# First latent scores ahead of the scan's last sums: query pairs issued inside the scan, the second half's output, norm and latents between the scores, the window masks on GpSimd

## The reference, cut to what matters

```python
# 4th part, cut: a linear recurrence over time
x_proj = x @ proj_in_w.T + proj_in_b
delta = softplus(x_proj @ B_w.T)                      # 16 states
h = h * sigmoid(A) + x_t[:, :, None] * d_t[:, None, :]  # scan over t
y_t = h.sum(axis=1) @ C_w.T + D_param * x_t
x = layernorm(x + (y @ proj_out_w.T + proj_out_b + x))
# 5th part, cut: cross-attention with latents, 16 heads
kv_c = kv @ W_kvc;  q_c = q @ W_dq
q = q_c @ W_uq, rope(q_c @ W_qr);  k, v from kv_c
good = (k_ids <= seg_id) & (k_ids >= seg_id - 8)
attn = softmax(where(good, q.k * scale, -1e30))
out = (attn @ v) @ W_o
```

## Time and profile before

| | us |
|---|---|
| median of 3 runs | 761.76 (760.17 to 761.87) |
| the profiled execution | 763.71 |
| its span, first to last instruction | 761.9 |
| TensorE busy in the span | 698.1 (92%) |
| VectorE busy | 485.4 (64%) |
| GpSimd busy | 318.7 (42%) |
| ScalarE busy | 305.6 (40%) |

### The profile page before, as it was taken

The page is one execution under the profiler, slowest core; times in us unless marked ns, Lnnn a source line. Parts: engine busy times, 40 slices in busy tenths (PEclk is TensorE's granted clock), DMA queues, the critical chain, the costliest instruction groups (busy, mean ns, idle before and its releaser), DMA issues.

```text
span 761.9 us, 12253 instructions
## 1 busy us (share of the span) xinstructions
PE 698.1 (92%) x4554; PEld 534.4 (70%) x4554; DVE 485.4 (64%) x928; ACT 305.6 (40%) x716; POOL 318.7 (42%) x453
## 2 busy tenths in 40 slices
PE   5989899999999898777999999999979999999993
PEld 4856564685666565435877787877858888888883
DVE  4478764331135789975998988882455656565656
ACT  3655523102211845122767776771142222222220
POOL 4323316400101769402766666662243445544521
PEclk9999999999799999887999999999979999999998
DMA  7000006001002000000000000003010111121001
GB/s 261 1 2 3 2 2 274 1 0 42 1 1 78 1 18 1 1 1 0 2 1 1 2 1 2 2 0 105 1 41 22 52 54 42 43 63 42 1 0 56
DMA packets 10460, 23.28 MB, mean 31 GB/s; under 512 B 2081, under 2 KB 5218, under 8 KB 10018
## 3 DMA queue, kind: packets, MB, share of 16 engines
q1 hardware_dynamic: 10402, 22.50, 8.9%
HBM read 21.45 MB, written 1.05 MB: 30 GB/s over the span
## 4 chain that ended last, share of the span: by engine, by line
PE 74%; DVE 18%; ACT 4%; issue 3%; DMA 1%; POOL 0%; POOLq 0%; DVEq 0%; SPq 0%; ACTq 0%
PE psum L394 30%; PE psum L427 8%; DVE A L1259 7%; PE psum L914 6%; PE psum L945 4%; PE psum L646 4%; PE psum L923 3%; PE psum L450 3%; PE psum L729 2%; PE psum L501 2%; PE psum L543 1%; DVE probs L1103 1%; DVE A L1170 1%; PE psum L507 1%; PE psum L407 1%
## 5 line engine op out<-in xcount | busy, mean ns | idle before, releaser
L394 PE MATMUL psum<-parts 128*128 128x256 f32 (+2 forms) x1440 | 255.8, 337 | 13.5 <-DVE parts L1124 8.7
L394 PEld LDWEIGHTS psum<-parts 128*128 128x128 f32 (+1 forms) x1440 | 221.4, 194 | 45.6 <-DVE parts L1124 8.7
L1710 POOL TENSOR_SCALAR probs<-probs,row_rec 128x256 f32<-128x256 f32 x128 | 60.8, 489 | 55.0 <-DVE row_rec L1114 53.9
L1433 ACT ACTIVATE probs<-probs,neg_max 128x256 f32<-128x256 f32 x128 | 64.0, 503 | 40.4 <-DVE neg_max L1107 40.4
L1259 DVE TENSOR_TENSOR_SCAN A<-decay,psum 128x256 f32<-128x256 f32 x128 | 75.0, 660 | 5.4 <-PE psum L774 5.4
L1660 ACT ACTIVATE A<-psum 128x512 f32<-128x512 f32 x44 | 26.3, 598 | 129.6 <-PE psum L394 129.6
L1380 DVE TENSOR_TENSOR A<-A,psum 128x512 f32<-128x512 f32 x44 | 30.2, 687 | 70.2 <-PE psum L394 70.2
L1826 POOL CAST parts<-C 128x512 fp32r<-128x512 f32 (+1 forms) x44 | 31.1, 707 | 100.5 <-PE psum L394 90.1
L914 PE MATMUL psum<-C,A 128*128 128x256 f32 x256 | 69.6, 396 | 0.0
L1827 POOL TENSOR_TENSOR parts<-C,parts 128x512 fp32r<-128x512 f32 (+1 forms) x44 | 54.9, 1247 | 3.5
L914 PEld LDWEIGHTS psum<-C,A 128*128 128x128 f32 x256 | 44.8, 194 | 15.6 <-issue 10.7
(11 more groups left out here) (206 smaller groups left out, 1191.1 us busy)
## 6 DMA issues: line engine op xcount, KB each, us to landing
C<-in_experts SPq DMA_DIRECT2D x22, 384.0 KB, 3.1
A<-in_w_o SPq DMA_DIRECT2D x1, 2048.0 KB, 12.0
x_tok<-in_x_tok SPq DMA_DIRECT2D x1, 1024.0 KB, 6.9
ctxT<-in_ctxT SPq DMA_DIRECT2D x1, 1024.0 KB, 10.4
out<-x_tok SPq DMA_DIRECT2D x8, 128.0 KB, 1.8
A<-in_w_uqT SPq DMA_DIRECT2D x1, 768.0 KB, 6.0
xT<-in_xT SPq DMA_DIRECT2D x2, 256.0 KB, 4.4
C<-in_wqk SPq DMA_DIRECT2D x1, 512.0 KB, 5.8
```

The costliest lines, as they stand in the source:

```text
L394: ins = mm(o, left[l], right[r], start=first and n == 0, stop=last and n == 2, skip_group_check=True)
L1433: last = af(slot, scores, ACT.Exp, bias=neg_max[:, u % RING[n], j:j + 1], accum_out=row_sum[:, u % RING[n], j:j + 1])
L1710: last = pool.tensor_scalar(pr, pr, row_rec[:, u % RING[n], j:j + 1], 1.0, ALU.mult, ALU.mult)
```

## The change

Pairs 0 to 2 are issued by TensorE in units 29 to 31 of the scan and pair 3 right behind; the scores begin when scan 62 of 64 is through. The last state sums and the second half's `outputs` come after `scores4(1)`, its output products after scores 2 and 3, its turn after scores 9, its query latents after scores 13. VectorE rotates pairs 0 and 1 inside the scan and does merge, residuals, norm and `query_low(1)` inside the attention. The eight masks are written by GpSimd in the odd units 7 to 21 of the scan, behind a wait for `k_tok`. `latents_by_token` turns the keys' latents instead of multiplying again. The first half's output products, norm, turn and latents come one unit earlier. ScalarE loads its exponential table in unit 20. The second half's sums go to a place of their own, and some PSUM banks change.

```diff
-        FIRST = 3
-        QUERIES_AT = {2 * (n - FIRST) + 1: n for n in range(FIRST, B * NPAIR)}
+        FIRST = 4
+        QUERIES_AT = {2 * (n - FIRST) + 4: n for n in range(FIRST, B * NPAIR)}
+        TURNS_AT, LATENTS_AT = 9, 13
 # TensorE
             def latents_by_token():
-                pe.wait_ge(sem("k_latT"), 2)
+                pe.wait_ge(sem("k_latT"), 4)
                 for i in range(NT):
-                    for c in range(DC):
-                        last = mm(bank[4][:, KVC * i:KVC * i + KVC],
-                                  ctxT[:, i // 2, c, (i % 2) * P:(i % 2 + 1) * P], w_kvc[:, c, 0:KVC],
-                                  start=(c == 0), stop=(c == DC - 1))
+                    last = pe.transpose(bank[4][:, KVC * i:KVC * i + KVC], keys_b[0:KVC, i * P:(i + 1) * P],
+                                        ident[0:KVC, 0:KVC])
...
-                if n == 22:
+                if n == 21:
                     final(3, (2, 3), out3)
-                if n == 26:
+                if n == 25:
                     ln_transposes(3, 0)
-                if n == 28:
+                if n == 27:
                     query_latents(0)
-            state_sums(7)
-            pe.wait_ge(sem("q_split"), 3)
-            pe.wait_ge(sem("operand_lo"), QC_AT + 1)
+                if n == 29:
+                    pe.wait_ge(sem("q_split"), 3)
+                    pe.wait_ge(sem("operand_lo"), QC_AT + 1)
+                if n >= 29:
+                    query_pair(n - 29)
+            query_pair(3)
+            def next_queries(u):
+                n = QUERIES_AT.get(u)
+                if u == 1:
+                    state_sums(7)
+                    outputs(1)
+                if u in (2, 3):
+                    if u == 2:
+                        pe.wait_ge(sem("q_mul"), 3)
+                    final(3, (2 * u, 2 * u + 1), out3)
+                if u == min(QUERIES_AT):
+                    pe.wait_ge(sem("ln_r"), 8 * 3 + NT)
+                if u == TURNS_AT:
+                    pe.wait_ge(sem("q_mul"), QUERIES_AT[u - 1] + 1)
+                    pe.wait_ge(sem("q_lat"), QUERIES_AT[u - 1] + 1)
+                    ln_transposes(3, 1)
+                if u == TURNS_AT + 1:
+                    pe.wait_ge(sem("ln_xT"), 4 * 3 + 4)
+                if u == LATENTS_AT:
+                    pe.wait_ge(sem("q_mul"), QUERIES_AT[u - 1] + 1)
+                    query_latents(1)
+                if u == LATENTS_AT + 1:
+                    pe.wait_ge(sem("operand_lo"), QC_AT + 2)
+                if n is not None:
+                    query_pair(n)
...
-            query_pair(0)
-            outputs(1)
-            query_pair(1)
-            pe.wait_ge(sem("q_mul"), 1)
-            final(3, range(4, NT), out3)
-            query_pair(2)
-            pe.wait_ge(sem("q_lat"), 3)
-            ln_transposes(3, 1)
-            query_latents(1)
-            pe.wait_ge(sem("q_mul"), 3)
+            pe.wait_ge(sem("s_scan"), 2 * SCAN_UNITS - 2)
             pe.wait_ge(sem("k_add"), 4)
 # VectorE, in the scan (residual3(2), (3) at m == 43, normalise at 47, query_low(0) at 57)
+                if m in (60, 62):
+                    rotate_pair((m - 60) // 2)
-            window_mask(0)
-            rotate_pair(0)
-            merge(1)
-            rotate_pair(1)
-            for i in range(4, NT):
-                residual3(i)
             rotate_pair(2)
-            for i in range(4, NT):
-                normalise(3, i)
-            window_mask(1)
-            query_low(1)
+            rotate_pair(3)
+            dve.wait_ge(sem("mask"), NT)
 # VectorE, rotate_next(u) of the attention
-                if u % 16 in (10, 12) and u < 16 * (B - 1):
-                    window_mask(2 * (u // 16) + 2 + u % 16 // 12)
+                if u == 1:
+                    merge(1)
+                if u in (2, 3):
+                    for i in (2 * u, 2 * u + 1):
+                        residual3(i)
+                if u == 5:
+                    for i in range(4, NT):
+                        normalise(3, i)
+                if u == LATENTS_AT:
+                    query_low(1)
 # ScalarE
+                if n == 20:
+                    af(small[:, 0, 0:1], small[:, 1, 0:1], ACT.Exp)
+                if n >= 30:
+                    latent_pair(n - 30)
+            latent_pair(2)
+            latent_pair(3)
             sums_out(1)
...
+                if u == TURNS_AT:
+                    ln_out(3, 1)
+                if u == LATENTS_AT:
+                    query_high(1)
 # GpSimd
+            def window_mask(i):
+                link(pool.tensor_scalar(distance, iota4, seg_f[:, i:i + 1], 1.0, ALU.subtract, ALU.mult))
+                link(pool.tensor_tensor(distance, distance, distance, ALU.mult))
+                pool.tensor_scalar(mask_m[:, i, :], distance, 16.0, NEG, ALU.is_gt, ALU.mult).then_inc(sem("mask"), 1)
+                pool.wait_ge(sem("mask"), i + 1)
-                if n == 25:
+                if n == 24:
                     rstd_of(3, (0,))
+                if n == 7:
+                    loaded(pool, "iota4", "seg")
+                    link(pool.tensor_copy(seg_f[:, :], seg_i[:, :]))
+                    pool.wait_ge(sem("k_tok"), 1)
+                if n % 2 and 7 <= n < 7 + 2 * NT:
+                    window_mask((n - 7) // 2)
+                if n == 31:
+                    add_pair(0)
...
+                if u == 4:
+                    rstd_of(3, (1,))
-            add_pair(0)
-            add_pair(1)
-            rstd_of(3, (1,))
-            add_pair(2)
+            for n in range(1, FIRST):
+                add_pair(n)
```

More of the change, by code:

```diff
@@ L792, in outputs @@
                     o = bank[(4, 2)[half] + c]
[L793 removed]
+                    mm(o[:, :], Cw2[:, c, :], zT[half], start=True, stop=True).then_inc(sem("s_y"), 1)
             def out3(i, o):
@@ L833, in query_latents, with query_pair @@
                 for c in range(DC):
-                    last = mm(bank[4 + 2 * half][0:QC, :], w_dq[:, c, :], xT[:, c, half * HALF:(half + 1) * HALF],
+                    last = mm(latent_bank(half)[0:QC, :], w_dq[:, c, :], xT[:, c, half * HALF:(half + 1) * HALF],
                               start=(c == 0), stop=(c == DC - 1))
                 last.then_inc(sem("qc"), 1)
+            def query_pair(n):
+                rhs = [qc_parts[:, r, n // NPAIR * S:(n // NPAIR + 1) * S] for r in range(2)]
+                p = n % NPAIR
+                rope, lat = q_banks(n)
+                if n:
+                    pe.wait_ge(sem("q_lat"), n)
+                if n >= 2:
+                    pe.wait_ge(sem("q_mul"), n if n > FIRST else n - 1)
+                left = lambda w: [w[:, r, p, :] for r in range(2)]
+                product3(rope[:, 0:S], left(wqr_raw_parts), rhs, True, True)
+                product3(rope[:, S:2 * S], left(wqr_swp_parts), rhs, True, True).then_inc(sem("q_rope"), 1)
+                product3(lat[:, 0:S], left(qk_parts), rhs, True, True).then_inc(sem("q_l"), 1)
             in_proj(0)
@@ L1280, in query_low, with rotate_pair @@
                 dve.wait_ge(sem("operand_hi"), QC_AT + half + 1)
-                tt(qc_parts[:, 1, hh], bank[4 + 2 * half][0:QC, :], qc_parts[:, 0, hh].bitcast(f32), ALU.subtract
+                tt(qc_parts[:, 1, hh], latent_bank(half)[0:QC, :], qc_parts[:, 0, hh].bitcast(f32), ALU.subtract
                    ).then_inc(sem("operand_lo"), 1)
+            def rotate_pair(n):
+                rope = q_banks(n)[0]
+                dve.wait_ge(sem("q_rope"), n + 1)
+                if n >= 2:
+                    dve.wait_ge(sem("q_add"), n - 1)
+                tt(ropes[:, n % 2, 0:S], rope[:, 0:S], tab_qc, ALU.mult)
+                tt(ropes[:, n % 2, S:2 * S], rope[:, S:2 * S], tab_qs, ALU.mult).then_inc(sem("q_mul"), 1)
             for w in range(2):
@@ L1298, in _ @@
                     residual3(1)
-                if m == 45:
+                if m == 43:
                     residual3(2)
                     residual3(3)
-                if m == 49:
+                if m == 47:
                     for i in range(4):
                         normalise(3, i)
-                if m == 59:
+                if m == 57:
                     query_low(0)
[L1308 to L1325, removed]
+                    loaded(dve, "tab_qc", "tab_qs")
+                if m in (60, 62):
+                    rotate_pair((m - 60) // 2)
             def rotate_next(u):
@@ L1565, in sums_out @@
                 act.wait_ge(sem("s_z"), 4 * (half + 1))
-                af(zT[:, half, :], bank[6 + half][:, :], ACT.Copy
+                if half:
+                    act.wait_ge(sem("q_split"), 2)
+                af(zT[half], bank[6 + half][:, :], ACT.Copy
                    ).then_inc(sem("s_zT"), 1)
@@ L1585, in query_high, with latent_pair @@
                 act.wait_ge(sem("qc"), half + 1)
```

(18 more changed lines are left out.)

49 lines of the change are left out of this document (9 added, 40 removed).

## The result

The changed kernel took 771.29 us (median of 5, 767.08 to 772.34) against 761.76 (5 runs) before: the medians lie 1.25% apart, and the ratio on record, with its interval, is 1.0101 (95%: 1.0067 to 1.0135). The five times of the changed kernel lie in two groups, near 767.2 and near 771.8, which differ in TensorE's mean granted clock (0.962 and 0.955) and not in the work; the profiled one is of the upper group, while the profiled execution before has 0.962. The forecast was 763, its own range 758 to 767, and with the rivals 754 to 769.

What follows compares the result with a forecast made beforehand. Bound: VectorE in the scan, nobody in the 24.7 us bridge, TensorE in the attention. Terms 10.9 - 23.0 + 10.5 - 3.1 + 2.9 + 2.8 = +1.0 gave about 763 us, range 758 to 767, with rivals 754 to 769.

Steps and rivals of the forecast that it cites:

- the price of a mask: GpSimd in the scan: a mask costs 1.9 us, bounds 1.5 and 2.5; seven before unit 20 cost 13.4.
- The third rival: Scan units 7 to 19: masks dear on GpSimd, 2.5 us each, giving 767, or 770 with longer attention waits; chance 0.29.
- The mechanism around it: Scan: GpSimd's 40.8 us of queued work from k_tok to unit 20's tiles makes unit 20 start +7.3 us later.
- The rival that GpSimd's lateness does not reach VectorE: Scan: unit 20 starts at 301.6, scan ends at about 337.5, time 752; chance 0.29 for 750 to 758.
- Output products at the lower clock: Scan behind unit 20: VectorE's residuals wait for TensorE's output products at half clock, +2.0 us.
- The rotations: Scan: two query rotations of 0.8 us now stand between scans on VectorE, the bound engine, +1.6 us.
- The latents by turns: Scan, before unit 7: eight turns replace sixteen products, so VectorE no longer waits, a gain of 1.9 us.
- The bridge: Scan's end to first masked score: 1.7 instead of 24.7 us, -23.0; work returning up to the seventh score, +10.5.
- The two uncovered waits: First to seventh masked score: first exponential and merge wait about 2.0 us, the norm for rstd about 1.9.
- Inside the attention: Masks leaving VectorE -3.1 us, turn and query latents on TensorE +2.9, new waits at units 9, 10 and 13 +2.8.
- The port lock: Scan: each GpSimd mask product holds a VectorE scan up, 5.8 us more, 769; chance 0.02.

Runs made afterwards that it cites:

- e3: The changed kernel with other forms of a mask's first and third operation in masks 0 to 4; one execution, 775.05 us.
- e4: The kernel before with only the masks moved to GpSimd, in the same units 7 to 21; 776.54 us, ratio 1.0165.
- e5: The changed kernel with the mask's first operation adding the negated segment number instead of subtracting it; 764.75 us, ratio 1.0022.
- e8: The changed kernel with all masks on VectorE, GpSimd still waiting for k_tok in unit 7; 756.04 us, ratio 0.9903.
- e2: The changed kernel with masks set to zero by one clearing operation in unit 24, the window of keys not applied; 753.52 us, ratio 0.9877.
- e9: The kernel before with only the latents by token turned from the keys' latents; 759.45 us, ratio 0.9954.
- e10: The changed kernel with masks on ScalarE and GpSimd taking the second half's rstd ahead of pair 4's add; 748.35 us, ratio 0.9813.
- e7: The changed kernel with masks 0 and 1 on GpSimd in units 21 and 25, the others on VectorE; 752.75 us, ratio 0.9877.
- e1: The changed kernel with all masks back on VectorE and without GpSimd's wait for k_tok; 754.49 us, ratio 0.9895.
- e6: The changed kernel with all masks on ScalarE in units 19 to 26, as a ramp that VectorE subtracts; 754.88 us, ratio 0.9884.

## Why the prediction was wrong, point by point

**The step that failed is the price of a mask.** I had it at 1.9 us, bounds 1.5 and 2.5, its first and third operation taken as a scaling. It was 3.1: a `tensor_scalar` of GpSimd that subtracts or compares (1.15 and 1.09 us) is not priced by one that multiplies (0.46; e3). The third rival had the place, the direction and the turning point (2.1 us) right, but its ceiling of 2.5 gave 767 to 770; it was given 0.29.

**The mechanism around it held.** 40.8 us of GpSimd's work from `k_tok` to unit 20's tiles, with seven masks at 3.1 instead of 1.9, are 49.2; from 269.31 to the end of the first two scalings of the row at 317.27 (half of its 1.84) are 48.9. e4, e5 and e8 give the same from three sides: the masks alone lose it, a cheaper operation gives it back nearly in proportion, and the wait alone loses nothing. So unit 20 came 15.5 us later behind the first scan than before (67.1 against 51.6), where I had 7.3. The rival that GpSimd's lateness does not reach VectorE is refuted; its 752 is near what the kernel takes when the masks are gone (e2, 753.5).

**Output products at the lower clock** were taken at +2.0 and cost 0.4: VectorE waited 0.27 us at residual 2 (row 326.73) and 0.14 before residual 0. The first turns were slow, as forecast, but the granted clock was back before 322 (0.57 in the window from 321), under 4 us behind the resumption at 318.30; before, work resumed at 315.64 and the window from 321 still shows 0.79. The products of the first pair took 2.79 and not 3.7.

**The rotations** were put at +1.6; each of the two held the next scan up by about 0.65 us, so 1.3. **The latents by turns** (-1.9) stand: e9 shows 1.9.

**The bridge** stood at -23.0 + 10.5 and came at -23.4 + 9.9. The two uncovered waits are there: 1.54 us for the first exponential (row 360.83) and 1.96 for rstd (row 375.12), and e10 shows that the second was worth 1.1 us of the time.

**Inside the attention** -3.1 + 2.9 + 2.8 became +1.3 in sum. The masks are right (e4: 143.2 instead of 146.2 us behind the seventh score), and so are turn and latents (1.07 + 1.96). Of the waits only the one at unit 9 came, 1.69 us in front of the turn; TensorE did not stand idle in units 10 and 13.

**The port lock** on scans is refuted: the 20 scans of the row at 296.16, beside masks, took 0.58 us each, as before, and no scan of the stage lasted longer than before (0.69 us at most in both). In the Trainium skill, SBUF — State Buffer, section "SBUF: two separate sides", the lock is for VectorE operations in a two-port mode or with two SBUF inputs. A scan here reads PSUM and, from SBUF, the decay alone, so by that rule the lock does not arise, and the trace agrees (0.58 us each).

With the measured prices the sum would have been 1.0 + 8.4, less 1.6 for the products, 0.3 for the rotations and 2.3 for bridge and attention: +5.2, as the landmarks gave, and a median of 767. That is where the changed kernel's two executions at the clock of the profile before (0.962) lie. The rest up to 771.29 is 2.4 us ahead of the scan and behind the attention, which nothing shows to be the change's, and the 1.95 us by which the profiled execution before lay above its median. Putting the mask's price alone right gives 763 + 8.4 = 771, on the measured median, but by luck: this leaves in 4.2 us of other terms that were too high.

## What to carry to other kernels

Price each operation on the engine that it is moved to, by its own arithmetic function: a row of the same instruction, shape and engine is no price if its function is another. Ask of work moved onto an engine with idle time what stands queued behind it up to the next point where somebody needs that engine, and add the fixed work of that stretch before comparing it with the time there is; a busy share over the stage (13.55 of 37.2 us here) does not tell. Where an engine's work is movable, try it where the slack is, or on the third engine: eight masks cost 18 us of scan in units 7 to 21 of GpSimd, two cost none in 21 and 25, and eight none on ScalarE. And before a difference of 2 us between two runs is given to an edit, compare the granted clock in that stretch: it made e7 look no better than e1.

## What the runs showed of the hardware that was not expected

GpSimd's `tensor_scalar` on 128 x 256 float32 took 0.41 to 0.48 us for multiply twice or add with multiply (0.41 with constants, 0.46 to 0.48 with a number per partition), 0.94 for a single subtraction, 1.07 to 1.15 for a pair with a subtraction, a maximum or a comparison, into float32 or bf16 alike. Its `tensor_tensor` took 0.61 to 0.62 us for a product or a subtraction there, and 0.73 for the bias, an addition. ScalarE's absolute value with a bias by partition and its ramp took 0.49 and 0.51 us for the same shape (e6), without a table load of their own. VectorE's four normalisations took 1.73 us in e6 and 2.28 in e10, where GpSimd's two-input additions (0.73 us each) ran beside them.
